# One target window per group of three edge blocks, and a node table normalised once: a two-layer graph network on one core

## The reference

```python
h = maximum(layernorm(x), 0)                           # x: 12500 nodes x 128
agg = segment_sum(h[src], dst)                         # 200000 edges, dst is sorted
x = x + agg @ W_rel.T + b_rel + h @ W_root.T           # layer 0
h = maximum(layernorm(x), 0)
w = silu(edge_attr @ We1 + be1) @ We2 + be2            # edge_attr: 200000 x 50
agg = segment_sum(h[src] * w, dst)
x = x + h + silu(agg @ Wn1 + bn1) @ Wn2 + bn2          # layer 1
```

## Time and profile before

| what | value |
|---|---|
| median of 3 runs | 4972.77 us (4953.61 to 4975.04) |
| profiled execution | 4927.46 us |
| its span, first to last instruction | 4925.0 us |
| instructions in the span | 49782 |
| mean granted TensorE clock | 0.638 |

### The profile page before, as it was taken

How to read it: one execution, slowest core, us unless ns; L and a number is a source line. 1 busy time by engine, 2 the same in 40 slices (tenths; PEclk the granted TensorE clock), 3 DMA queues, 4 the chain that set the end, 5 groups by cost and what they waited for, 6 DMA issues and landing times.

```text
span 4925.0 us, 49782 instructions
## 1 busy us (share of the span) xinstructions
PE 2588.1 (53%) x10958; PEld 1971.2 (40%) x10958; DVE 1954.1 (40%) x6931; ACT 1186.6 (24%) x2732; POOL 2980.9 (61%) x3135
## 2 busy tenths in 40 slices
PE   1333333333333333333436768677777777676777
PEld 0333333333333332333324445455545455454555
DVE  3344444443444444444523333333333333333334
ACT  1333333333333333333401111111111111111111
POOL 7566666666666666666265666666666666665662
PEclk9555555555555555555556777766777777767777
DMA  2111211112111121111122222222222222222221
GB/s 70 49 49 53 55 49 50 50 52 54 50 51 50 50 57 51 49 50 50 35 61 62 65 68 68 65 64 64 68 64 68 62 66 69 67 64 63 67 68 53
DMA packets 205872, 285.33 MB, mean 58 GB/s; under 512 B 67828, under 2 KB 135462, under 8 KB 205618
## 3 DMA queue, kind: packets, MB, share of 16 engines
q0 software_dynamic: 100096, 205.20, 16.1%
q10 hardware_dynamic: 62434, 61.11, 4.3%
q1 hardware_dynamic: 43216, 17.95, 1.4%
HBM read 263.58 MB, written 20.45 MB: 58 GB/s over the span
## 4 chain that ended last, share of the span: by engine, by line
another core or an unknown queue 30%; PE 26%; DVE 18%; issue 17%; DVEq 5%; ACT 4%; ACTq 0%; DMA 0%; POOL 0%; SPq 0%; POOLq 0%
PE seg_a L305 8%; PE seg_b L305 4%; DVE e_stats L588 4%; PE ew_a L351 4%; DVEq L579 3%; PE ew_b L351 3%; PE hid_a L345 3%; PE hid_b L345 3%; ACT rows L413 2%; DVE onehot L572 2%; DVE e_mv L592 2%; DVE agg L583 2%; DVE ew_a L673 1%; DVE rows L680 1%
## 5 line engine op out<-in xcount | busy, mean ns | idle before, releaser
L276 POOL DMA_INDIRECT rows<-h_rows,idx x1564 | 1490.9, 953 | 976.4 <-issue 537.7
L276 POOL DMA_INDIRECT rows<-x,idx x1564 | 1489.0, 952 | 892.7 <-issue 479.7
L305 PE MATMUL seg_a<-onehot,rows 128*128 128x128 f32 x3312 | 746.7, 397 | 1354.3 <-ACT rows L413 514.4
L305 PEld LDWEIGHTS seg_a<-onehot,rows 128*128 128x128 f32 x3312 | 657.7, 295 | 1447.1 <-issue 1141.1
L305 PE MATMUL seg_b<-onehot,rows 128*128 128x128 f32 x2944 | 626.5, 381 | 572.6 <-DVE onehot L572 269.7
L413 ACT ACTIVATE rows<-rows,e_shift,e_rstd 128x128 f32<-128x128 f32 x1564 | 643.3, 481 | 907.8 <-DVE e_shift L599 719.8
L305 PEld LDWEIGHTS seg_b<-onehot,rows 128*128 128x128 f32 x2944 | 557.0, 282 | 648.6 <-issue 461.9
L572 DVE TENSOR_TENSOR onehot<-iota_ps,dst_rel 128x512 f32<-128x512 f32 x782 | 532.5, 681 | 1.4
L583 DVE TENSOR_TENSOR agg<-seg_a,agg 128x128 f32 x414 | 119.8, 289 | 760.4 <-remote 393.3
L494 ACT ACTIVATE hidden<-hid_a,be_col 128x512 f32<-128x512 f32 x208 | 142.9, 687 | 1137.4 <-remote 522.6
L351 PEld LDWEIGHTS ew_a<-we_sb,hidden 128*128 128x128 f32 x1664 | 272.8, 248 | 309.0 <-ACT hidden L494 184.2
(11 more groups left out here) (102 smaller groups left out, 1712.4 us busy)
## 6 DMA issues: line engine op xcount, KB each, us to landing
rows<-x,idx POOLq DMA_INDIRECT x1564
rows<-h_rows,idx POOLq DMA_INDIRECT x1564
ef_a<-ef_blocks ACTq DMA_DIRECT2D x70, 300.0 KB
ef_b<-ef_blocks ACTq DMA_DIRECT2D x47, 300.0 KB
xs<-x SPq DMA_DIRECT2D x26, 256.0 KB
y_rows<-ys ACTq DMA_DIRECT2D x26, 256.0 KB
ys<-y_rows SPq DMA_DIRECT2D x26, 256.0 KB
out<-xs ACTq DMA_DIRECT2D x26, 256.0 KB
```

The source lines that it names most:

```text
L276: pool.indirect_dma_start(out=rows[:, u, t, :], out_offset=None, in_=table, in_offset=bass.IndirectOffsetOnAxis(ap=idx[:, j:j + 1], axis=0 ...
L305: mm = pe.matmul(seg[u % 2][:, 0:P], rows[:, u, t, :], onehot[:, u % HOT, t, :], start=(t == 0), stop=(t == TB - 1))
```

## The change

Both layers work in groups of three blocks (the last group of an iteration has two), so six groups take the place of 17 blocks:

- one window base per group, taken as the minimum over its blocks, with one range of 128 nodes for 1536 edges;
- one comparison of 1536 columns (1024 for the short group) makes the 0/1 matrices of the group, in two buffers where there were three;
- the 12 (8) matmuls of a group accumulate in one PSUM bank, and `s_seg` is raised once per group; the landings of a group's gathers share one semaphore (`s_rows[layer][g]`);
- `add_window` runs once per group, one group late, and on over the loop's turn: the last sum of an iteration is added in the next;
- POOL waits once per group, for the same group of the iteration before.

Layer 0 also normalises each node once. A loop ahead of the layer (5 rounds of 5 sets of 512 nodes) loads `x`, takes statistics, applies the ReLU, stores the result to the new table `h_rows` in DRAM, and keeps its transpose in the SBUF room of `agg[1]`. Iteration 0 still gathers raw rows and normalises each edge, since the table is not ready. Iterations 1 to 22 gather from `h_rows`, and TensorE sums the rows as they land. The node update of layer 0 no longer has its first statistics, ReLU and transposes; it runs in iterations 1 to 22, with three late groups as before. The clearing of `agg[0]` now comes after the loop on VectorE.

The core of the diff:

```diff
+GB = 3
+G = -(-U // GB)
-        onehot = sb("onehot", [P, HOT, TB, P])
+        onehot = sb("onehot", [P, 2, GB * TB, P])
...
+            with sp.Fori(0, GROUPS // H_SETS - 1) as k:
+                for r in range(H_SETS):
+                    store_h(k, r)
+                    load_h(k + 1, r)
...
+            def gather(layer, table, i, loads):
+                for g in range(G):
...
+                    hold(pool, s_seg[layer], i * G + (g + 1))
+                    for u in blocks_of(g):
+                        for t in range(TB):
...
             with pool.Fori(0, passes_so_far) as p:
-                with pool.Fori(0, ITERS) as it:
-                    gather(0, x, p * ITERS + it, 0)
+                gather(0, x, p * ITERS, p * ITERS)
+                for r in range(H_SETS):
+                    hold(pool, s_hstore[r], 16 * (GROUPS // H_SETS + 1))
+                with pool.Fori(1, ITERS) as it:
+                    i = p * ITERS + it
+                    gather(0, h_rows, i, i)
...
             def segment_sum(layer, u):
+                g, k = u // GB, u % GB
+                last = u == blocks_of(g)[-1]
                 for t in range(TB):
-                    mm = pe.matmul(seg[u % 2][:, 0:P], rows[:, u, t, :], onehot[:, u % HOT, t, :],
-                                   start=(t == 0), stop=(t == TB - 1))
-                mm.then_inc(s_seg[layer], 1)
+                    mm = pe.matmul(seg[g % 2][:, 0:P], rows[:, u, t, :], onehot[:, g % 2, k * TB + t, :],
+                                   start=(k == 0 and t == 0), stop=(last and t == TB - 1))
+                if last:
+                    mm.then_inc(s_seg[layer], 1)
...
+            with dve.Fori(0, GROUPS // H_SETS) as k:
+                def stats_h(r):
+                    dve.wait_ge(s_hx[r], k * 16 + 16)
+                    stats_of(h_x[r], r, s_hbn, k * H_SETS + (r + 1), s_hstats)
...
+                stats_h(0)
+                for r in range(H_SETS):
+                    if r + 1 < H_SETS:
+                        stats_h(r + 1)
+                    shift_of(r, s_hstd, s_hrecip, s_hshift, k * H_SETS + (r + 1))
+                    if r >= 2:
+                        copy_h(r - 2)
             v.memset(agg[0][:, :], 0.0)
...
+                with dve.Fori(1, ITERS) as it:
                     i = p * ITERS + it
...
+                    for g in range(G):
+                        if g > 0:
+                            add_window(0, i, it, g - 1)
+                        else:
+                            add_window(0, i - 1, it - 1, G - 1)
+                        one_hot(it + (g + 1) // G, (g + 1) % G).then_inc(s_onehot, 1)
+                        if g in steps:
+                            steps[g]()
...
+            def edge_blocks(i, it, first):
...
+                for u in range(U):
+                    g, k = u // GB, u % GB
+                    message(i, u)
+                    if k == 1:
+                        if g > 0:
+                            add_window(1, i, it, g - 1)
+                        elif not first:
+                            add_window(1, i - 1, it - 1, G - 1)
+                        one_hot(it + (g + 1) // G, (g + 1) % G)
+                    if u + 1 < U:
+                        edge_bias(i, u + 1)
```

538 lines of the change are left out of this document (311 added, 227 removed).

## The result

| | before | changed |
|---|---|---|
| median of 4 runs each | 4965.75 us (4953.61 to 4975.04) | 4850.14 us (4848.64 to 4858.36) |
| profiled execution | 4927.46 us | 4849.66 us |
| its span | 4925.0 us | 4847.9 us |
| instructions | 49782 | 35780 |
| mean granted TensorE clock | 0.638 | 0.665 |

The ratio is 0.9764, 95% interval [0.9741, 0.9787]: faster by 2.4%, where the forecast said 5.7% (4691 us).

The account below looks back on a forecast made before the run. POOL's gathers, plus holes where POOL waits for signals that arrive late while it issues unbroken, bound the kernel. 4927 - 288 + 65 - 59 = 4645; of the median, 4973 - 282 = 4691 us; range 4450 to 4990.

Parts of the forecast that it names:

- The start: Normalising loop ahead of layer 0: POOL stands until the table is stored, gathers resume at about 172 us; +65 us.
- The end of layer 0: POOL's stand between the layers: two groups at most left (-51) and a shorter late update (-8); -59 us.
- Layer 1: Layer 1's loop: fewer adds and signals, but POOL released in steps of three blocks; 0, bounds -115 and +360 us.
- rival C: Layer 1: POOL's release in steps of three blocks lengthens its holes, +360 us, 5051 us in all; chance 0.14.
- Steady layer 0: Iterations 2 to 22 of layer 0: 90 us each in place of 103.7, fewer signals per gather; -288 us.
- The lower bound of 85.1: Layer 0, one iteration: 68 gathers at 1.25 us with no hole of POOL's left.
- 97 us in layer 0: The forecast with 97 us an iteration in steady layer 0: -139 in place of -288, 4840 us; chance 0.10.
- The reading of the bound: Whole kernel: while POOL issues without a break, signals between other engines arrive late; a pause of POOL lets them through.
- Rival B: Steady layer 0: nothing gained, the holes may belong to the gathers' own pace; 4979 us, no change; chance 0.08.
- Rivals A: Both layers: the gathers bind outright, 85.1 us in layer 0, layer 1 five us less; 4474 us; chance 0.20.
- D: Both layers: a group's targets span over 128 nodes, so every layer is passed over twice; under one in a hundred.
- The rules: Code fetch at layer 0's loop turn (2.84 us, 60 us at most); VectorE's clearing harmless to gathers, or costing ten us.

Follow-up runs that it names:

- e15: Changed kernel with layer 0 in stretches (six pauses, three, empty instructions, half sums, unchanged), layer 1 by groups, blocks, blocks with pauses; 4158.16 us against 3993.07 before.
- e16: The same kernel as e15 once more, in a set of runs with the freeze; 4771.12 us against 4912.58 for the kernel before.

## Why the prediction was right or wrong

**The start: right** (+65 forecast, +66.4; gathers resumed at 174.3 for 172, iteration 2 at 273.3 for 272). Its cause is the freeze: without it the normalising loop runs beside the gathers of iteration 0, and POOL goes on at 102 to 108. The mechanism was right as well: VectorE began to clear `agg[0]` at 143.87, where the forecast had the last set at 141.

**The end of layer 0: the size was right, the way to it partly luck** (-59 forecast, -53.8). The forecast had at most two groups left after POOL's last gather, and 15 us for them. TensorE's timeline after the last gather, at 2320.03:

```profile
2324.57 4.80 PE L370 MATMUL seg_a<-onehot,rows 128*128 128x128 f32 x22 [1.03 <-issue]
2329.21 2.84 PE L370 MATMUL seg_b<-onehot,rows 128*128 128x128 f32 x24
2331.89 2.84 PE L370 MATMUL seg_a<-onehot,rows 128*128 128x128 f32 x24
2336.57 2.05 PE L370 MATMUL seg_b<-onehot,rows 128*128 128x128 f32 x16 [1.84 <-DVE onehot L711]
```

Four groups were left, eleven blocks, so POOL was twice as far ahead as forecast. But with POOL at rest a group took under 5 us on average and not 7.5, and all four were through after 18.6 us (the 17 blocks before took 67). The late update, from there to the first gather of layer 1, took 29.2 us in place of 34.4.

**Layer 1: a small miss** (0 forecast, +39.1, inside the bounds -115 to +360). If it is rival C's mechanism, it is so at an eighth of its price or less (1 to 2 us an iteration for the release, where C had 15.6). Why the price is so small is open: layer 1 stands longer per gather than the debt, so the debt does not explain it.

**Steady layer 0: the step that failed** (-288 forecast, -128.9). The sentence was "the signals needed per gather fall far more than the signals' lateness could grow". It took lateness as a property of a signal, 12 to 20 us at most, read where POOL had issued 51 gathers in one go. The traces show a lateness that grows while POOL does not stand: with fewer stops VectorE's waits grew to 35 and 40 us, the time from a sum to its signal from 7 us to 25 and 43, and the holes from about 3 us to 6. Two stops an iteration in place of six or seven left POOL standing 12.6 us an iteration, where it had stood 18.8 and the forecast had 5. The row that spoke of it was at hand: before, VectorE waited 20 us after a long run of gathers and 6 after a short one. The lower bound of 85.1 was nowhere near on this chip; the lowest stretch there took 96.8 us (95.0, if only the four iterations with half of the sums are counted). The case "97 us in layer 0" gave 4840 us, 10 below the result, with a chance of 0.10. Its chance was low because I had no mechanism for it; that it stood there at all was a guess. Two small slips changed nothing: the earlier trace rows give 1.27 us between two sets, where the prediction reads 1.26, and 97 us in layer 0 make -141, not -139.

**The reading of the bound** ("a pause of POOL lets them through") held. "Signals arrive late" was too narrow: weight loads and matmuls without a semaphore between them are held up as well. Rival B (nothing gained in steady layer 0) fell on this chip; on chips without the freeze, no gain is what the runs of its near relatives show. Rivals A and D fell.

**The rules.** At the turn of layer 0's loop VectorE no longer stands 2.84 us. The last instruction of one iteration and the first of the next:

```profile
1516.01 0.73 DVE L765 TENSOR_TENSOR ys<-xs,node_work 128x512 f32<-128x512 f32 x1
...
1516.66 0.28 DVE L723 TENSOR_TENSOR agg<-seg_b,agg 128x128 f32 x1
```

The add has no idle time before it, with a loop body of 77 instructions. By the rule of the Trainium skill (Runtime: NRT & Kernel Launch, Instruction fetch mechanics) a jump stalls when its target lies outside the current two pages, and so short a body lies inside; this trace agrees. But I find none of the 60 us in the sum: layer 0 took what the gathers and their holes took. The first gather of layer 1 again took 12.30 us beside the clearing of `agg[1]`, with and without the freeze. The Trainium skill (SBUF — State Buffer, Who interferes with whom) says that a VectorE instruction with at most one SBUF input, outside the two-port modes, does not contend with GpSimd; these rows do not fit it. They are not a test of it either, since no run left the clearing out, and the first clearing, in the trace before (13.85 to 24.57 us), is less plain: the three gathers that began in its first 4 us took 0.94 to 0.95 us each, and only the next was long.

```profile
18.69 7.23 POOL L276 DMA_INDIRECT rows<-x,idx  x1 [0.30 <-issue]
```

## What to carry to other kernels

Where POOL issues indirect DMAs back to back, look at what the other engines start in a stretch without a hole before you count on their shorter work: if even instructions without a semaphore come us apart, expect a floor of the issue time plus the holes per gather (here 1.25 + 0.18 us). Nothing that was tried here got clearly below it; fewer gathers should, which no run tried. Take a lateness as a rate (us of hole per gather since the last hole), not as a constant, and try it against runs of different length in the same trace. And time the kernel before beside every experiment: the same program took 3993 us in one set of runs and 4966 in another, and the change was worth 2.4% in the second, while its near relatives were worth nothing in the first.

## What was not expected of the hardware

- The freeze is there in some sets of runs and absent in others, with the same program: three sets with it (before 4966, 4908, 4913 us), and all others without (before 3992 to 4000 us). e15 and e16 are the same kernel: 4158 us without it, 4771 with it.
- With it, all engines but POOL went down to six matmuls, five weight loads and nothing else in 27 us, while the gathers keep their 1.25 us and the DMA its 53 GB/s.
- A gather costs POOL 0.95 us for 128 rows, 0.90 for 64 and 0.86 for 32.
- The four traces with the freeze hold 15020 to 18771 records of semaphore updates, and the sixteen without it 59681 to 60205. For the same kernel they are 60006 (e15) and 17718 (e16).

What the freeze is stays open. No run here shows the mechanism. The last point is the nearest hint: the kernel's waits need every one of these updates, 16 for each gather, so with the freeze it is records that are missing, and not updates (a profile then puts waits down to "remote" or "issue"). The freeze comes together with a loss of records. Whether one causes the other, or something else causes both, no run tells. The Trainium skill (NOTIFIC — the notification-queue block, Instances and attachment) describes one unit per core that takes the records of all engines and of semaphore events; under The write path it says that its internal pipeline holds the engines back rather than lose a record. The engines held back would fit it, the missing records would not. Whether that is the place was not tried, since no edit here took records of the gathers away. The times of this document come with spans and clocks out of such records, so whether an execution without them has the freeze, and whether the change is worth anything there, is open too. Open, too: the gain of the release by blocks in both layers with the freeze, and the changed kernel itself on a chip without it (its nearest, released by blocks in layer 1, took 3998.22 and 3998.80 us against 3992.98 and 3991.99).
